# Transformer block with routed experts on one core: a setup that waits only for the front loop's loads, x loaded and its first norm taken inside it, the attention branch's weights split beside the routing, and a zero fill read from one row

## The chip, the cores and the metric

One of a Trainium2 chip's eight cores runs the kernel. Its engines are TensorE (PE in the rows), VectorE (DVE), ScalarE (ACT), GpSimd (POOL) and SyncE (SP), which here only issues transfers. The metric is the device time of one execution in microseconds, the median of several runs; lower is better.

## What is computed

`x` is 4 sequences of 2048 tokens with 256 features, 8192 tokens in all. The core of the reference normalises it and feeds it to two branches:

```python
xn = _layernorm(x, axis=-1)
s = _L0_attn_ref(xn, ...)     # linear attention, convolution, MLP of 1024
g = _silu(_L0_ffn_ref(xn, ...))   # attention over the 4 sequences' tokens, then 16 experts
x = x + s * g
```

`_L0_ffn_ref` takes a layer norm of `xn`, projects it to q, k, v (16 heads, 4 key/value heads), attends among the four tokens that share a position, projects and adds, takes a second layer norm `ln2`, and computes 16 router logits per token. Each token goes to its two best experts, into a slot of a buffer with 1280 slots per expert (unused slots are zero); each expert is an MLP 256 to 512 to 256; the results are weighted with the routing's probabilities and added. `_L0_attn_ref` needs `Wq, Wk, Wv`, `Wphi_q, Wphi_k`, a grouped convolution `conv_w` scaled by `gamma`, and an MLP `W1` (256x1024), `W2` (1024x256). All is float32.

## The kernel before

The program is written by hand, engine by engine, in blocks. Within a block each engine runs its own list, and semaphores tie the lists together; at the end of a block all engines meet before the next one starts. `Chain` makes each step of a list wait for the one before it. The blocks are, in order:

1. **Setup** (lines 264 to 424). SP issues 20 loads, then 16 small ones that place `conv_w` block by block into `wconv` (line 340); ScalarE issues 13 loads of vectors (line 353). All 33 count on one semaphore, `loaded`. POOL clears `wconv`, `brow2` and `zeros`, loads `wrouter`, and builds ten masks. VectorE waits for `loaded` and for the masks (`masks_made`), makes `bcast` and `one_rows` (lines 399 to 401), and TensorE computes sums of weight columns from them (lines 377 to 388); when all are done (`sums_made`), VectorE folds norm weights and means into `wqkv` and `wrouter` (lines 413, 414) and builds rows of biases `brow`. The weights of the attention branch are split into a high and a low part for exact products: `w_hi` by ScalarE, `w_lo = w - w_hi` by VectorE (`wa`, `w1`, lines 420, 422) or POOL (`w2`, line 310). POOL also scales `wconv` by `gamma` (line 306) and adds the identity (line 308), and scales `wphi` (line 314). Last, SP copies the split biases into `brow2` (lines 345, 346).
2. **Front loop** (lines 477 to 803), 16 turns, each with 4 x 128 tokens (one tile of each sequence). It is software-pipelined: in turn t, VectorE takes the statistics of x(t) (`front_stats`, lines 723 and 726), POOL turns them into the scale and shift of the two norms in eight steps (`norm`, lines 504 to 522), ScalarE applies them a turn later (`xn`, line 562, `xn_twice`, line 584), TensorE transposes and projects (line 708), and the attention among four tokens and the second norm follow two to four turns behind. SP loads x(t) into one of two buffers (line 484) once ScalarE is done with x(t-2), and after each x it issues one sixteenth of the zero fill of the experts' buffer `buf_d`, from a tile `zeros` of 128 x 10 x 272 (line 486). Each row of 272 holds 256 features and tags, one of which is a mark for an empty slot.
3. **Routing** (lines 827 to 898). VectorE alone finds the two best experts of all 8192 tokens in 13 steps on 128x1024 tiles, up to `chosen` (line 873); TensorE counts; VectorE computes slots. ScalarE takes two exponentials. POOL has no work.
4. **Attention branch** for sequences 0 and 1 with the scatter of tokens to the experts, **experts**, and the attention branch for sequences 2 and 3 with the final mix.

Before the routing's end, nothing of block 4 uses `wa_s`, `w1_s`, `w2_s`, `wphi`, `wconv` or `b1c`. `xnb` (128 x 16 x 256) holds normed rows of the attention branch; its first four tiles are written at the front loop's end.

The code that sets what a turn of the feed does:

```python
                            if later(t, 2):
                                sp.wait_ge(xn_made, t.n * S - S)
                            sp.dma_start(x[t.odd][:], rows_of(a["x"], t)).then_inc(x_in[t.odd], 16)
```

## Time and profile before

| | us |
|---|---|
| median of 3 runs | 2023.04 (2022.46 to 2023.44) |
| the profiled execution, its own time | 2030.76 |
| its span in the trace | 2029.0 |
| setup, up to the front loop's first issue | 48.0 |
| first `xn` of the front loop | 58.07 |
| routing, first step of VectorE | 366.39 |
| routing, last step of VectorE | 393.98 |

The trace is of one execution. Its own time is 1.8 us more than its span (what lies around the first and the last instruction) and 7.7 us more than the median of the runs. Times in the rows count from the span's start. An engine's busy time says what it worked, not what the others waited for; for that one reads which wait ended last in a stretch.

### The profile page before, as it was taken

To read this page: it belongs to the slowest core of one execution; us is meant where nothing else is said; L and a number is where in the kernel's file an instruction comes from. 1 tells how busy PE (TensorE), PEld (TensorE's weight loads), DVE (VectorE), ACT (ScalarE), POOL (GpSimd) and SP (SyncE) were. 2 spreads that over 40 slices of the span, in tenths; PEclk is the share of its full clock that TensorE was granted. 3 is DMA by queue.
4 is the path that set the end of the run, shared out by engine and by line. 5 is a ranking of instruction groups with operands and counts; after the bars stand their busy time and mean duration, and the time that the engine had idled before them with its cause. 6 is when DMAs were issued, how large, how long until landed. Compare 5 with 4: busy or idle time off the path is not lost. (4 is left out here: it accounts for less than half of the span.)

```text
span 2029.0 us, 37231 instructions
## 1 busy us (share of the span) xinstructions
PE 1812.5 (89%) x12776; PEld 1620.9 (80%) x12776; DVE 1375.7 (68%) x3573; ACT 817.8 (40%) x1945; POOL 962.0 (47%) x1500
## 2 busy tenths in 40 slices
PE   2699998399999999996999999999888999998998
PEld 2377776285898867996999999999875799875998
DVE  2698885654556535553777778877567588794786
ACT  1466664163323553321333333333355333572332
POOL 4466663175555564553656656566342233330431
PEclk9999999599999998997999999999989999998999
DMA  3454432123333123332333343332145022361122
GB/s 97 186 181 174 171 138 74 51 76 114 139 131 129 62 96 126 114 131 84 110 115 124 100 135 126 94 122 74 48 123 177 22 79 65 111 196 31 53 66 63
DMA packets 163510, 218.29 MB, mean 108 GB/s; under 512 B 22874, under 2 KB 144931, under 8 KB 161294
## 3 DMA queue, kind: packets, MB, share of 16 engines
q1 hardware_dynamic: 140574, 166.61, 25.7%
q0 software_dynamic: 18464, 49.49, 6.9%
q8 instruction: 97, 1.59, 0.3%
q10 hardware_dynamic: 4304, 0.02, 0.1%
q14 instruction: 71, 0.58, 0.1%
HBM read 114.94 MB, written 107.22 MB: 109 GB/s over the span
## 5 line engine op out<-in xcount | busy, mean ns | idle before, releaser
L1840 POOL DMA_INDIRECT picked_d<-h,home x160 | 163.6, 1022 | 192.3 <-DVE h L1887 156.7
L1766 ACT ACTIVATE hid<-bank 128x512 f32<-128x512 f32 x160 | 95.6, 598 | 336.1 <-PE bank L130 336.1
L128 PE MATMUL bank<-rows_hi,up_hi 128*128 128x256 f32 x640 | 189.0, 295 | 11.9 <-POOL up_lo L1834 7.6
L130 PE MATMUL bank<-rows_hi,up_lo 128*128 128x256 f32 x640 | 182.5, 285 | 0.0
L129 PE MATMUL bank<-rows_lo,up_hi 128*128 128x256 f32 x640 | 182.3, 285 | 0.0
L130 PE MATMUL bank<-down_hi,hid_lo 128*128 128x256 f32 x640 | 181.2, 283 | 0.0
L129 PE MATMUL bank<-down_lo,hid_hi 128*128 128x256 f32 x640 | 181.1, 283 | 0.0
L128 PE MATMUL bank<-down_hi,hid_hi 128*128 128x256 f32 x640 | 181.1, 283 | 0.0
L1170 POOL DMA_INDIRECT buf_d<-lt,to_row x128 | 134.4, 1050 | 86.4 <-POOL lt L1166 43.4
L1469 PE MATMUL bank<-wconv,knt 128*128 128x128 f32 x1280 | 157.1, 279 | 0.0
L1901 DVE TENSOR_TENSOR hid_lo<-hid,hid_hi 128x512 fp32r<-128x512 f32 x160 | 119.1, 753 | 52.6 <-ACT hid_hi L1766 49.8
L1469 PEld LDWEIGHTS bank<-wconv,knt 128*128 128x128 f32 x1280 | 152.6, 196 | 0.0
L1152 POOL TENSOR_SCALAR cnorm<-cmv 128x1 f32<-128x1 f32 x64 | 15.0, 235 | 289.9 <-DVE cmv L1672 289.0
L129 PE MATMUL bank<-w_lo,gel_hi 128*128 128x256 f32 x512 | 147.5, 288 | 0.0
L128 PE MATMUL bank<-w_hi,gel_hi 128*128 128x256 f32 x512 | 147.3, 288 | 0.0
L130 PE MATMUL bank<-w_hi,gel_lo 128*128 128x256 f32 x512 | 147.2, 288 | 0.0
L128 PE MATMUL bank<-ant_hi,w_hi 128*128 128x256 f32 x512 | 145.5, 284 | 0.0
L1334 ACT ACTIVATE tk<-bank,b1c 128x256 f32<-128x256 f32 x256 | 107.1, 471 | 90.4 <-PE bank L130 87.7
L129 PE MATMUL bank<-ant_lo,w_hi 128*128 128x256 f32 x512 | 143.0, 279 | 0.0
L130 PE MATMUL bank<-ant_hi,w_lo 128*128 128x256 f32 x512 | 142.9, 279 | 0.0
L1691 DVE TENSOR_TENSOR gel_lo<-tk,gel_hi 128x256 fp32r<-128x256 f32 x256 | 128.8, 503 | 8.8
L128 PEld LDWEIGHTS bank<-rows_hi,up_hi 128*128 128x128 f32 x640 | 124.1, 194 | 13.0 <-POOL up_lo L1834 8.0
(314 smaller groups left out, 5585.6 us busy)
## 6 DMA issues: line engine op xcount, KB each, us to landing
buf_d<-zeros SPq DMA_DIRECT2D x16, 1360.0 KB, 7.0
rows_in<-buf_d SPq DMA_DIRECT2D x80, 272.0 KB, 2.8
lt<-ln_d SPq DMA_DIRECT2D x128, 128.0 KB, 2.2
picked_d<-nothing SPq DMA_DIRECT2D x32, 512.0 KB, 3.3
job_picked<-picked_d SPq DMA_DIRECT2D x64, 256.0 KB, 2.9
x<-in_x SPq DMA_DIRECT2D x16, 512.0 KB, 4.3
after_d<-after SPq DMA_DIRECT2D x16, 512.0 KB, 2.9
ln_d<-ln SPq DMA_DIRECT2D x16, 512.0 KB, 2.8
```

The source lines that it names most:

```text
L128: pe.matmul(dst, hi, mhi, start=start and i == 0, stop=False)
L129: pe.matmul(dst, hi, mlo, start=False, stop=False)
L130: mm = pe.matmul(dst, lo, mhi, start=False, stop=end)
L1152: step.also(pool.tensor_scalar(n[3], mv_[0], -1.0, None, ALU.mult))
L1170: pool.indirect_dma_start(buf_d, bass.IndirectOffsetOnAxis(to_row[:, job, k:k + 1], axis=0), lt[p][:, k], None, bounds_check=SLOTS - 1, oo ...
L1334: act.activation(gel[:, f % 4], bank[f // 2 % 2][:, f % 2 * PAIR * P:(f % 2 + 1) * PAIR * P], ACT.Gelu, bias=b1c[:, f:f + 1]).then_inc(gel ...
L1469: mm = pe.matmul(conv[:, j * P:(j + 1) * P], attnt[:, j, k * P + tap:k * P + tap + P], wconv[:, j, tap], start=False, stop=j == 1 and tap ...
L1691: dve.tensor_tensor(lo[:, f], gel[:, f % 4], hi[:, f], ALU.subtract).then_inc(gel_split, 1)
L1766: act.activation(dst[:, 2 * half:2 * half + 2].rearrange("p f c -> p (f c)"), bank[half][:], ACT.Gelu_apprx_tanh).then_inc(e_hid, 1)
L1840: pool.indirect_dma_start(picked_d, bass.IndirectOffsetOnAxis(home[i % TAG_RING][:, r:r + 1], axis=0), h2[p][:, r], None, bounds_check=PIC ...
L1901: dve.tensor_tensor(lo[:, part], hid[p][:, part], hi[:, part], ALU.subtract).then_inc(hid_split, 1)
```

## The change

* **Loads.** They are reordered and count on three semaphores: `front_in` (`wqkv`, `wproj`, four vectors), `small_in` (19: `wphi`, biases, `gamma`, the other vectors) and `loaded` (8: `wa`, `w1`, `w2`, three rows). x(0) is loaded first of all and x(1) after the small ones, so that the loop's SP list issues x only from turn 2 on (`if later(t, 2)`).
* **Setup.** VectorE waits for `front_in` and two steps of POOL; it takes the statistics of x(0) there, and POOL its norm (`norm_twice`, the eight steps of lines 504 to 522 as a function), ahead of clearing `brow2` and `zeros`. Turn 0 of the loop has no statistics and no norm.
* **Splits.** The work on `wa`, `w1`, `w2`, `wphi`, `wconv` and `b1c` moves into the routing's block: ScalarE and TensorE do what they did; POOL does all four kinds of its own and both splits that were VectorE's. `w1` and `wa` stay in memory until then; `w2` lies in the last eight tiles of `xnb`.
* **Zero fill.** `zeros` is one row of 272 per partition, and the transfer reads it ten times.

```diff
-        zeros = sb("zeros", [P, CAP // P, ROW], into=front_only)
-        tags_made, zero_fill = sem("tags_made"), sem("zero_fill")
+        zeros = sb("zeros", [P, ROW], into=front_only)
+        zero_fill = sem("zero_fill")
+        w1 = sb("w1", [P, HALVES, MLP], into=front_only)
+        w2 = xnb[:, BT - MLP // P:BT]
+        wa = sb("wa", [P, HALVES, 3 * E], into=front_only)
+        gamma = sb("gamma", [P, 1], into=front_only)
+        x = [sb(f"x{p}", [P, S, E], into=front_only) for p in range(2)]
+        stats = sb("stats", [P, S, 6], into=front_only)
+        mv = [sb(f"mv{p}", [P, S, 2], into=front_only) for p in range(2)]
+        norm = [sb(f"norm{p}", [P, 8, S], into=front_only) for p in range(2)]
+        x_in = [sem("x_in0"), sem("x_in1")]
+        x_stats, x_mv, x_norm = sem("x_stats"), sem("x_mv"), sem("x_norm")
+        loaded, conv_in, pool_step = sem("loaded"), sem("conv_in"), sem("pool_step")
+        act_step, wa_high, sums_made = sem("act_step"), sem("wa_high"), sem("sums_made")
+        X_NORM = 8
+        LOADS, FRONT_LOADS, SMALL_LOADS, MASK_STEPS = 8, 6, 19, 20
...
-            LOADS = 33
...
-                    pool.memset(wconv[:], 0.0).then_inc(conv_blank, 1)
-                    pool.memset(brow2[:].bitcast(F32), 0.0).then_inc(rows_blank, 1)
-                    pool.memset(zeros[:], 0.0).then_inc(zeroed, 1)
-                    pool.wait_ge(zeroed, 1)
-                    pool.memset(zeros[:, :, E + 1], float(FAR)).then_inc(zeroed, 1)
...
-                    for t in (ident, diag, headmask, headmask_t, tri, earlier, ones_f, ones_b):
-                        step(pool.memset(t[:], 1.0))
-                    step(pool.memset(neg_half[:], -0.5))
-                    step(pool.memset(one_col[:], 1.0))
+                    for t in (ones_f, neg_half, ident, diag, headmask, headmask_t, tri, earlier, ones_b, one_col):
+                        step(pool.memset(t[:], -0.5 if t is neg_half else 1.0))
+                    pool.memset(wconv[:], 0.0).then_inc(conv_blank, 1)
...
+                              allow_small_or_imprecise_dtypes=True)
+                    assert step.done == MASK_STEPS
+                    pool.wait_ge(x_mv, S)
+                    norm_twice(pool, Chain(pool, x_norm), mv[0][:, :, 0], mv[0][:, :, 1], norm[0])
+                    pool.memset(brow2[:].bitcast(F32), 0.0).then_inc(rows_blank, 1)
+                    pool.memset(zeros[:], 0.0).then_inc(zeroed, 1)
+                    pool.wait_ge(zeroed, 1)
+                    pool.memset(zeros[:, E + 1:E + 2], float(FAR)).then_inc(zeroed, 1)
...
+                    def load(dst, src, done):
+                        sp.dma_start(dst, src).then_inc(done, 16)
+
+                    sp.dma_start(x[0][:], rows_of(a["x"], Step(0, 0))).then_inc(x_in[0], 16)
+                    load(wqkv[:], a["qkv_t"].rearrange("(j p) n -> p j n", p=P), front_in)
+                    load(wproj[:], a["proj_t"].rearrange("(j p) n -> p j n", p=P), front_in)
+                    load(wphi[:, 0], a["Wphi_q"].rearrange("(j p) n -> p j n", p=P), small_in)
+                    load(wphi[:, 1], a["Wphi_k"].rearrange("(j p) n -> p j n", p=P), small_in)
+                    for i, name in enumerate(("bq", "bk", "bv")):
+                        load(brow[:, i * E:(i + 1) * E], row(a[name]), small_in)
+                    for i, name in enumerate(("bphi_k", "conv_b", "lna_b", "b2")):
+                        load(extra[:, i * E:(i + 1) * E], row(a[name]), small_in)
+                    load(gamma[:], a["gamma"].to_broadcast((P, 1)), small_in)
+                    sp.dma_start(x[1][:], rows_of(a["x"], Step(0, 1))).then_inc(x_in[1], 16)
                     for i, name in enumerate(("Wq", "Wk", "Wv")):
+                        load(wa[:, :, i * E:(i + 1) * E], a[name].rearrange("(j p) n -> p j n", p=P), loaded)
+                    load(w1[:], a["W1"].rearrange("(j p) n -> p j n", p=P), loaded)
+                    load(w2, a["W2"].rearrange("(j p) n -> p j n", p=P), loaded)
                     for dst, name in ((gv_row, "lnv_g"), (bv_row, "lnv_b"), (ga_row, "lna_g")):
+                        load(dst[:], row(a[name]).to_broadcast((P, E)), loaded)
...
-                    act.wait_ge(loaded, 16 * LOADS)
+                    act.wait_ge(small_in, 16 * SMALL_LOADS)
                     act.activation(phik_zero[:], bphi[:, 1], ACT.Tanh).then_inc(phi_zero, 1)
-
-                    step = Chain(act, act_step)
-                    step(act.activation(w2_s[0][:], w2[:], ACT.Copy))
-                    act.activation(wa_s[0][:], wa[:], ACT.Copy).then_inc(wa_high, 1)
-                    act.wait_ge(sums_made, 1)
-                    for j in range(HALVES):
-                        step(act.activation(w1[:, j], w1[:, j], ACT.Copy, scale=lna[:, 0, j:j + 1]))
-                    step(act.activation(w1_s[0][:], w1[:], ACT.Copy))
...
-                        pe.matmul(bank[1][:, 0:P], bcast[:, 1, j], wrouter[:, j], start=j == 0, stop=j == 1)
+                        last = pe.matmul(bank[1][:, 0:P], bcast[:, 1, j], wrouter[:, j], start=j == 0, stop=j == 1)
+                    last.then_inc(sums_made, 1)
+                    pe.wait_ge(small_in, 16 * SMALL_LOADS)
...
-                    dve.wait_ge(loaded, 16 * LOADS)
+                    dve.wait_ge(front_in, 16 * FRONT_LOADS)
                     dve.wait_ge(router_in, 16)
-                    dve.wait_ge(masks_made, 1)
...
+                    dve.wait_ge(x_in[0], 16)
+                    for k in range(S):
+                        dve.bn_stats(stats[:, k], x[0][:, k]).then_inc(x_stats, 1)
+                    dve.wait_ge(x_stats, S)
+                    for k in range(S):
+                        dve.bn_aggr(mv[0][:, k], stats[:, k]).then_inc(x_mv, 1)
...
+                    dve.wait_ge(small_in, 16 * SMALL_LOADS)
+                    dve.wait_ge(sums_made, 2)
...
-                    dve.wait_ge(wa_high, 1)
-                    dve.tensor_tensor(wa_s[1][:], wa[:], wa_s[0][:], ALU.subtract).then_inc(wa_high, 1)
-                    dve.wait_ge(act_step, 4)
-                    dve.tensor_tensor(w1_s[1][:], w1[:], w1_s[0][:], ALU.subtract).then_inc(w1_split, 1)
...
-                            sp.dma_start(x[t.odd][:], rows_of(a["x"], t)).then_inc(x_in[t.odd], 16)
+                                sp.dma_start(x[t.odd][:], rows_of(a["x"], t)).then_inc(x_in[t.odd], 16)
 
                             sp.dma_start(buf_d.rearrange("(x p n) e -> p x n e", x=NX, p=P)[:, bass.ds(t.n, 1)]
-                                         .rearrange("p x n e -> p (x n) e"), zeros[:]).then_inc(zero_fill, 16)
+                                         .rearrange("p x n e -> p (x n) e"),
+                                         zeros[:].unsqueeze(1).to_broadcast((P, CAP // P, ROW))).then_inc(zero_fill, 16)
...
+                @block.gpsimd
+                def _(pool):
+                    step = Chain(pool, pool_step, MASK_STEPS)
+                    pool.wait_ge(loaded, 16 * LOADS)
+                    pool.wait_ge(wa_high, 1)
+                    pool.tensor_tensor(wa_s[1][:], wa[:], wa_s[0][:], ALU.subtract).then_inc(wa_high, 1)
+                    for i, g in enumerate((lnq, lnk)):
+                        for j in range(HALVES):
+                            step(pool.tensor_scalar(wphi[:, i, j], wphi[:, i, j], g[:, 0, j:j + 1], None, ALU.mult))
+                    pool.wait_ge(conv_in, 16 * H)
+                    step(pool.tensor_scalar(wconv[:], wconv[:], gamma[:, 0:1], None, ALU.mult))
+                    for j in range(HALVES):
+                        step(pool.tensor_tensor(wconv[:, j, 2], wconv[:, j, 2], ident[:], ALU.add))
+                    pool.wait_ge(act_step, 1)
+                    step(pool.tensor_tensor(w2_s[1][:], w2, w2_s[0][:], ALU.subtract))
+                    pool.wait_ge(act_step, 4)
+                    step(pool.tensor_tensor(w1_s[1][:], w1[:], w1_s[0][:], ALU.subtract))
+
                 @block.tensor
                 def _(pe):
+                    pe.wait_ge(loaded, 16 * LOADS)
+                    for n in range(MLP // P):
+                        for j in range(HALVES):
+                            last = pe.matmul(bank[4][:, n:n + 1], w1[:, j, n * P:(n + 1) * P], lna[:, 1, j:j + 1],
+                                             start=j == 0, stop=j == 1)
+                    last.then_inc(sums_made, 1)
...
+                    step = Chain(act, act_step)
+                    act.wait_ge(loaded, 16 * LOADS)
+                    act.activation(wa_s[0][:], wa[:], ACT.Copy).then_inc(wa_high, 1)
                     act.wait_ge(route_step, SHIFTED)
                     act.activation(odds[:], logit, ACT.Exp).then_inc(odds_made, 1)
+                    step(act.activation(w2_s[0][:], w2, ACT.Copy))
                     act.wait_ge(route_step, SECOND + 1)
                     act.activation(second[:], second[:], ACT.Exp).then_inc(second_made, 1)
+                    act.wait_ge(sums_made, 3)
+                    for j in range(HALVES):
+                        step(act.activation(w1[:, j], w1[:, j], ACT.Copy, scale=lna[:, 0, j:j + 1]))
+                    step(act.activation(w1_s[0][:], w1[:], ACT.Copy))
...
+                    dve.wait_ge(sums_made, 3)
+                    step(dve.tensor_tensor(b1c[:], bank[4][:, 0:MLP // P], b1c[:], ALU.add))
```

POOL's list. The setup before, from its second wait for the loads to its end (`w` is `w2`, `bank` a PSUM bank):

```order
L301 IOTA rank_e 128x16 [waits pool_step]
L306 TENSOR_SCALAR wconv<-wconv,gamma 128x1280 [waits conv_in,loaded]
L308 TENSOR_TENSOR wconv<-wconv,ident 128x128 [waits pool_step] x2
L310 TENSOR_TENSOR w_lo<-w,w_hi 128x2048 [waits act_step,pool_step]
L314 TENSOR_SCALAR wphi<-wphi,lnq 128x256 [waits sums_made,pool_step]
L314 TENSOR_SCALAR wphi<-wphi,lnq 128x256 [waits pool_step]
```

and after, the whole of POOL's list in the routing's block, which was empty before:

```order
L828 TENSOR_TENSOR wa_lo<-wa,wa_hi 128x1536 [waits wa_high,loaded]
L831 TENSOR_SCALAR wphi<-wphi,lnq 128x256
L831 TENSOR_SCALAR wphi<-wphi,lnq 128x256 [waits pool_step]
L831 TENSOR_SCALAR wphi<-wphi,lnk 128x256 [waits pool_step] x2
L833 TENSOR_SCALAR wconv<-wconv,gamma 128x1280 [waits conv_in,pool_step]
L835 TENSOR_TENSOR wconv<-wconv,ident 128x128 [waits pool_step] x2
L837 TENSOR_TENSOR w_lo<-xnb,w_hi 128x2048 [waits act_step,pool_step]
L839 TENSOR_TENSOR w_lo<-w,w_hi 128x2048 [waits act_step,pool_step]
```

The rows of the setup stand in the routing with both subtracts of VectorE's added: `wa_lo` first, the one of `w1` last (the name `xnb` is the place of `w2`).

VectorE's list in the setup before:

```order
L399 TENSOR_SCALAR bcast<-ones_f,ln1b,ln1w 128x128 [waits masks_made,router_in,loaded]
L401 CAST one_rows<-ones_f 128x128 [waits setup_step]
L404 COPY router_bias<-bank 128x16 [waits sums_made,setup_step]
L408 TENSOR_SCALAR brow<-extra,gamma 1x256 [waits setup_step]
L409 TENSOR_TENSOR brow<-extra 1x256 [waits setup_step]
L414 SCALAR_TENSOR_TENSOR wqkv<-bank,wqkv 128x384 [waits setup_step]
L416 CAST brow_hi<-brow 1x1536 [waits setup_step]
L418 TENSOR_TENSOR brow_lo<-brow,brow_hi 1x1536 [waits rows_split]
L420 TENSOR_TENSOR wa_lo<-wa,wa_hi 128x1536 [waits wa_high]
L422 TENSOR_TENSOR w_lo<-w,w_hi 128x2048 [waits act_step]
L424 TENSOR_SCALAR phik_zero<-phik_zero 128x2 [waits phi_zero]
```

and after:

```order
L406 TENSOR_SCALAR bcast<-ones_f,ln1b,ln1w 128x128 [waits pool_step,router_in,front_in]
L408 CAST one_rows<-ones_f 128x128 [waits setup_step]
L411 BN_STATS stats<-x 128x6 [waits x_in0,setup_step]
L414 BN_AGGR mv<-stats 128x2 [waits x_stats]
L417 COPY router_bias<-bank 128x16 [waits sums_made]
L421 SCALAR_TENSOR_TENSOR wqkv<-bank,wqkv 128x384 [waits setup_step]
L425 TENSOR_TENSOR phiq_bias<-bank,bphi 128x2 [waits sums_made,small_in,setup_step]
L427 TENSOR_SCALAR brow<-extra,gamma 1x256 [waits setup_step]
L428 TENSOR_TENSOR brow<-extra 1x256 [waits setup_step]
L429 CAST brow_hi<-brow 1x1536 [waits setup_step]
L431 TENSOR_TENSOR brow_lo<-brow,brow_hi 1x1536 [waits rows_split]
L433 TENSOR_SCALAR phik_zero<-phik_zero 128x2 [waits phi_zero]
```

The statistics of x stand where `one_rows` used to be followed by the wait for all sums; the two splits are gone; the wait for the small loads comes after the folds of `wqkv` and `wrouter`.

SP's list at the end of the setup and the start of the loop, after:

```order
L360 DMA brow<-brow_hi 1x16x96 [waits rows_blank,rows_split,zeroed]
L361 DMA brow<-brow_lo 1x16x96
L288 UNCONDITIONAL_BRANCH [waits row_two]
L478 UNCONDITIONAL_BRANCH [waits barrier_Pool_Activation_PE_DVE_SP_release]
L486 DMA buf_d<-zeros 1280x1x272 x2
L484 DMA x<-in_x 128x4x256 [waits xn_made]
L486 DMA buf_d<-zeros 1280x1x272
```

Before, the same two `brow` copies were followed by `x`, fill, `x`, fill, and the fill's form was 128x2720.

## Rows read from the trace of the kernel before

**Rows 1.** The page, busy time of each engine.

```profile
PE 1812.5 (89%) x12776; PEld 1620.9 (80%) x12776; DVE 1375.7 (68%) x3573; ACT 817.8 (40%) x1945; POOL 962.0 (47%) x1500
```

**Rows 2.** By stage: start:end, length, busy PE, PEld, DVE, ACT, POOL; PEclk, DMA share, GB/s.

```profile
0.00:48.00 48.00, 13.99 (x52) 11.22 (x52) 12.63 (x22) 8.97 (x7) 24.69 (x39) 1.00 0.37 96
110.00:200.00 90.00, 87.85 (x474) 65.68 (x473) 79.55 (x215) 59.54 (x127) 54.19 (x99) 1.00 0.50 180
366.30:382.70 16.40, 0.00 (x0) 0.00 (x0) 15.90 (x13) 1.31 (x2) 0.00 (x0) 0.50 0.00 0
```

**Rows 3.** Timeline of ScalarE, first `xn` and two turns: start, length, line, operation.

```profile
58.07 2.07 ACT L562 ACTIVATE xn<-x,norm 128x256 f32<-128x256 f32 x4 [17.94 <-POOL norm L505]
...
104.33 2.08 ACT L562 ACTIVATE xn<-x,norm 128x256 f32<-128x256 f32 x4 [2.01 <-PE bank L646]
...
120.97 2.08 ACT L562 ACTIVATE xn<-x,norm 128x256 f32<-128x256 f32 x4 [2.11 <-PE bank L646]
```

**Rows 4.** Waits up to 62 us: who waited for whom, us.

```profile
PE bank L377 <- DVE one_rows L401: 21.8, 1, 21.8
...
DVE bcast L399 <- DMA ga_row<-in_lna_g: 20.1, 1, 20.1
...
SPq L344 <- DVE brow_lo L418: 20.2, 1, 20.2
```

**Rows 5.** Timeline of VectorE, setup and first turns.

```profile
45.17 2.27 DVE L422 TENSOR_TENSOR w_lo<-w,w_hi 128x2048 fp32r<-128x2048 f32 x1
...
52.14 1.41 DVE L723 BATCH_NORM_STATS2 stats<-x 128x6 f32<-128x256 f32 x4 [3.73 <-DMA x<-in_x]
...
70.43 1.40 DVE L723 BATCH_NORM_STATS2 stats<-x 128x6 f32<-128x256 f32 x4
```

**Rows 6.** Timeline of the SP queue: last large load, `wconv`, second `brow` copy, first x.

```profile
12.58 0.43 SPq L320 DMA_DIRECT2D ga_row<-in_lna_g  x1
13.06 10.30 SPq L340 DMA_DIRECT2D wconv<-in_conv_t  x16
...
44.28 0.59 SPq L346 DMA_DIRECT2D brow<-brow_lo  x1
48.01 0.39 SPq L484 DMA_DIRECT2D x<-in_x  x1
```

**Rows 7.** Transfers up to 12 us by queue, and up to 62 us by issue (last: us to landing).

```profile
q1 hardware_dynamic: 2137, 2.86, 71.4%
...
buf_d<-zeros SPq DMA_DIRECT2D x3, 1360.0 KB, 7.0
...
x<-in_x SPq DMA_DIRECT2D x3, 512.0 KB, 4.2
...
brow<-brow_lo SPq DMA_DIRECT2D x1, 6.0 KB, 1.8
```

**Rows 8.** Timeline of TensorE in the setup, the first and the last sums.

```profile
21.83 2.93 PE L377 MATMUL bank<-wqkv,bcast 128*128 128x384 f32 x4 [21.83 <-DVE one_rows L401]
...
28.84 6.99 PE L388 MATMUL bank<-lna,w 128*128 128x1 f32 x32
```

**Rows 9.** Timeline of POOL in the setup, and of VectorE beside its last rows.

```profile
24.98 3.57 POOL L306 TENSOR_SCALAR wconv<-wconv,gamma 128x1280 f32<-128x1280 f32 x1 [10.90 <-DMA wconv<-in_conv_t]
...
29.70 4.51 POOL L310 TENSOR_TENSOR w_lo<-w,w_hi 128x2048 fp32r<-128x2048 f32 x1
36.00 2.04 POOL L314 TENSOR_SCALAR wphi<-wphi,lnq 128x256 f32<-128x256 f32 x2 [1.79 <-PE bank L388]
...
37.37 0.50 DVE L409 TENSOR_TENSOR brow<-extra 1x256 f32<-1x256 f32 x1
```

**Rows 10.** Timeline of VectorE, then of POOL, in the expert stage.

```profile
1062.88 0.69 DVE L1880 TENSOR_TENSOR rows_lo<-rows_t,rows_hi 128x512 fp32r<-128x512 f32 x1
...
1069.78 2.77 DVE L1880 TENSOR_TENSOR rows_lo<-rows_t,rows_hi 128x512 fp32r<-128x512 f32 x1
...
1069.47 2.53 POOL L1834 TENSOR_TENSOR down_lo<-down_w,down_hi 128x1024 fp32r<-128x1024 f32 x1
```

**Rows 11.** Timeline of VectorE in the routing: the 2nd and 13th of 13 steps.

```profile
367.65 1.22 DVE L860 TENSOR_REDUCE highest<-logits 128x64 f32<-128x1024 f32 x1
...
381.47 1.22 DVE L873 TENSOR_TENSOR chosen<-hot 128x1024 bf16<-128x1024 f32 x1
```

97 lines of the change are left out of this document (30 added, 67 removed).

## The prediction

> **What bounds the kernel now.** I read the engine totals first. TensorE is busy 89% of the span [rows 1], so most of the 2029 us is its work and stays out of this change, which touches three stretches only: the setup, the front loop's feed and the routing. A table by stage shows how they differ [rows 2]. In the first 48 us no engine is busy for more than 25 us: this stretch is bounded by waits. In the front loop (110 to 200 us) TensorE is busy 87.85 of 90 us: there only TensorE's work counts, and a turn takes 120.97 - 104.33 = 16.64 us [rows 3]. In the routing's first 16.4 us VectorE is busy 15.90 us, POOL (GpSimd) not at all and TensorE not at all: VectorE is the bound, alone.
>
> Next, the waits of the setup. VectorE starts only at 20.14 us, when the last of all 33 loads has landed; TensorE at 21.83 us; the sync queue waits 20.2 us for `brow_lo` [rows 4]. VectorE's last long step is the split of W1, 45.17 to 47.44 us [rows 5], and the next block's first load is issued at 48.01 us [rows 6]. From there the first norm is a bare chain: x lands, statistics at 52.14 us [rows 5], POOL's eight small steps, and ScalarE's first `xn` at 58.07 us [rows 3]. That is 10.06 us in which only one thing happens at a time.
>
> **The change, part by part.**
>
> *Term 1, the end of the setup.* VectorE now waits for six loads, ahead of which stands only x: 512 + 384 + 256 KB, 1.18 MB. In the first 12 us the sync queue moved 2.86 MB [rows 7], so these should land at about 8 to 9 us (2 us until traffic flows, 1.18 / 0.286 = 4.1 us, some 2 us to landing, which is the 1.8 us of the tiny `brow_lo` transfer [rows 7]). What follows is short: VectorE's busy time in the whole setup was 12.63 us [rows 2], of which the splits of Wa and W1 leave (2.27 us the larger one [rows 5]), so even with the new statistics (under 2 us), TensorE's first sums, 21.83 to 25.6 us before, and its two small products, 3.6 us more up to 28.84 us [rows 8], VectorE is through at about 22 to 23 us. POOL had 24.69 us of work [rows 2]; 3.57 us of `wconv`, about 1 us of its identity, 4.51 us of W2's split and 4.04 us of `wphi` leave [rows 9], about 2 us of zeroing go with the smaller tile, 4 us of norm come: about 16 us of work with one wait, through at 20 us. So neither of them ends the setup. **The sync queue does**: its loads were all issued at 13.0 us [rows 6], with two x loads of 0.4 us more at 13.9 us; the 16 small `wconv` loads take 10.30 us of issuing [rows 6], to 24.2 us; the two `brow` copies take 0.6 us each, the second is issued at 24.8 us, lands 1.8 us later [rows 7] at 26.6 us, and from there to the next block's first issue it was 48.01 - 47.5 = 0.5 us. That is 27.1 us. The two x loads add 1.05 MB to a queue that was full when it issued; at 0.286 MB per us that is up to 3.7 us more of waiting. I take 0.5 us of it, since most of it is drained while the `wconv` loads are issued: 27.6 us, a gain of 20.4 us (bounds 17 to 21).
>
> *Term 2, the first norm.* It is now ready before the block starts, at about 13 us by VectorE and 17 us by POOL, below the setup's end. ScalarE's first `xn` starts as the block does, at 27.7 us instead of 58.07 us. Terms 1 and 2 together: -30.4 us. If the setup ends late, the second term stays at 10.0.
>
> *Term 3, the third x.* The first two turns of the new loop issue the zero fills alone, and x for turn 2 comes behind both, about 2.2 us after the block starts (when four `xn` are made). Its statistics were taken at 70.43 us [rows 5], 12.36 us after the first `xn`. A fill landed after 7.0 us and x after 4.2 us beside it [rows 7]. Two fills are 2.8 MB; as 2560 pieces at 64 ns on 16 queues (the setup's mean piece: 0.714 x 16 x 12 us / 2137 [rows 7]) they take 10.2 us, x 2 us more and landing 2 us: 14.7 us against 12.4. By the rate at which the larger pieces flowed it is in time. I take 1.0 us late (0 to 3).
>
> *Term 4, the splits beside the routing.* All of Wa, W1, W2, `wphi` and `wconv` now lies in the block where VectorE alone is the bound. ScalarE's part and TensorE's 16 sums (6.99 us for both halves, at most twice that at the granted clock of 0.50 that this stretch has [rows 2, 8]) run beside it and end before the 16.4 us are over: hidden, nothing queued behind them. POOL's part is not free, though POOL sits idle there. In the expert stage VectorE's `rows_lo`, two inputs in SBUF, takes 0.69 us; issued 0.3 us into POOL's subtract of 128x1024 it took 2.77 us and ended 0.5 us after POOL's [rows 10]. So it didn't run slower, it stood still. Of VectorE's 13 steps up to `chosen` nine are of that kind, 1.22 us each, and four are reduces with one input [rows 11]; the front loop's reduces don't stretch beside POOL. POOL's two-input steps here are `wa_lo`, 1536 columns at 4.51 / 2048 us [rows 9], 3.4 us; `wconv` plus identity, 2 x 0.45; `w2_lo` and `w1_lo`, 4.51 us each: 13.3 us. I lay them beside VectorE's steps (times from the block's start; `chosen` ended at 16.3 before). `wa_hi` is ready at 1.5, so `wa_lo` runs 1.6 to 4.95; VectorE's reduce ends at 2.5, and its next step waits to 4.95: 2.4 us lost. `wphi` and `wconv`, one input each, run to 12.8; the two identity steps cost 0.3. `w2_lo` runs 15.6 to 20.1, VectorE waits from 16.5: 3.6 lost. `w1_lo` has waited behind VectorE's step and takes its turn at 21.3, to 25.8: `chosen` waits, 4.4 lost. Sum 10.7 us, and 0.2 for `b1c` at the end: **+10.9 us** (bounds 0 if the steps don't stop one another here, and 13.5 if every us of it is lost).
>
> The Trainium skill, "SBUF — State Buffer", section "SBUF: two separate sides", says that the pair of ports which VectorE shares with GpSimd is an exclusive lock, held for the whole instruction, and it names any GpSimd instruction as a holder, not the two-input ones alone. By that rule POOL's one-input steps would stop VectorE too. The trace agrees on the two-input case with its 2.77 us [rows 10].
>
> What would one-input steps cost? `wphi` (4 x 0.98) and `wconv` (3.57) laid in the same way move `chosen` from 27.0 to 32.0: +5 us. The one row that bears on it speaks against: VectorE's two-input `brow` on `extra` ran from 37.37 to 37.87 us, inside a `wphi` step of POOL's that went on to 38.04 [rows 9]; 0.50 us is no stall of that length. I leave it out.
>
> *The fill from one row* changes nothing in the steady loop: 1280 pieces of 1088 bytes at 64 ns are 5.1 us of the queues in a turn of 16.64 us, where all traffic took half the time [rows 2]. The loads moved in order, the smaller memsets and the wait by `loaded` inside the routing cost nothing: all long landed.
>
> **Sum.** -30.4 + 1.0 + 10.9 = -18.5 us. The profiled execution took 2030.76 us, so 2012.3 us; the median of the runs is 7.7 us below it, 2023.04, so 2004.5 us is forecast. A measurement tells about 0.2% (4 us) from nothing.
>
> **The rivals.**
> 1. *No stall in the routing*, because the two-input steps meet mostly reduces, or because broadcast operands (most of the routing's) don't take the port. For it: in the front loop POOL's and VectorE's small steps alternate at little cost. Against: 2.77 us [rows 10]. It gives 2004.5 - 10.9 = 1993.6 us.
> 2. *Every POOL step stops VectorE*: 2004.5 + 5.0 = 2009.5 us.
> 3. *The setup ends late*: the change doesn't deliver its early start, since the loads it waits for share the 16 queues with all that is issued behind them, and the `wconv` loads and `brow` copies queue behind 1.05 MB more. The queues' data then ends 3.7 us later, and with the third x 2 us later than taken: 2010 us.
> 4. *The fill binds the loop* (the other side). 128 pieces of 10,880 bytes become 1280 of 1088. All traffic takes 8.3 us of a turn now; to lose the 18.5 us and 4 more, the turn must reach 16.64 + 22.5 / 16 = 18.0 us, so the fill would need 9.7 us more, 121 ns per piece. It decides from there; the setup's pieces took 64 ns. At 150 ns a turn takes 8.3 + 12 = 20.3 us, 59 us more in 16 turns: 2064 us.
>
> **How the numbers follow.** Forecast 0.62 (its own range 2000 to 2009). Rival 1: 0.13. Rival 2: 0.13. Rival 3: 0.08. Rival 4: 0.04. The range 1992.5 to 2012.5 holds the first four but for their tails. Only the fill can undo the gain, and a mild case of it would land near no change: faster 0.96, same 0.01, slower 0.03.
>
> **What would show it.** Step 1: the loop's first fill is issued near 27.6 us, right after the second `brow` copy has landed. Step 2: ScalarE's first `xn` within 0.3 us of it, and no idle before it. Step 3: VectorE's third statistics wait for x, by 0 to 3 us. Step 4: `chosen` ends 27 us after the routing's start, with three VectorE steps of 3.6, 4.8 and 5.6 us in place of 1.22, each ending 1.2 us after a POOL subtract. The forecast is wrong in its reasons if those steps stay at 1.22 us, if a reduce stretches, if the turn isn't 16.6 us, or if the expert stages' times move.

## The result, and the profile after

| | before | after |
|---|---|---|
| median of 15 runs each, us | 2022.46 (2015.51 to 2029.54) | 2013.95 (2009.12 to 2018.82) |
| profiled execution: its own time, span | 2030.76, 2029.0 | 2010.27, 2008.5 |
| front loop's first issue | 48.01 | 32.27 |
| first `xn` | 58.07 | 32.29 |
| routing, VectorE's first step | 366.39 | 343.26 |
| attention branch, TensorE's first product | 394.76 | 383.81 |

The changed kernel takes 0.9956 of the time before, 95% interval 0.9943 to 0.9969: 8.9 us less (6.3 to 11.5), where 18.5 us less was forecast. Runs of one kernel lie up to 18 us apart (2014.14 to 2032.53 us for the kernel before, beside run 1), and in the traces of all kernels here the time behind the attention branch's first product is between 1619 and 1634 us, whatever the kernel. So the two profiled executions, 20.5 us apart, are compared only up to that product. Up to there the change gains 394.76 - 383.81 = 10.95 us, in line with the medians: 25.8 up to the first `xn`, less 2.65 lost in the loop (308.32 us from first `xn` to routing before, 310.97 after), less 12.2 in the routing (28.37 us, now 40.55).

Busy time of each engine after (against [rows 1]), from the page:

```profile
PE 1806.9 (90%) x12775; PEld 1616.4 (80%) x12776; DVE 1382.0 (69%) x3571; ACT 818.0 (41%) x1945; POOL 968.5 (48%) x1502
```

By stage after: setup, a stretch of the loop, the routing up to `chosen` (against [rows 2], same columns):

```profile
0.00:32.20 32.20, 7.28 (x20) 4.32 (x20) 10.08 (x27) 1.49 (x2) 13.57 (x39) 0.77 0.63 175
110.00:200.00 90.00, 86.28 (x459) 63.78 (x458) 78.94 (x214) 58.39 (x124) 56.44 (x101) 1.00 0.55 176
343.20:371.60 28.40, 6.96 (x32) 6.90 (x32) 27.90 (x14) 8.69 (x7) 24.91 (x10) 0.50 0.00 1
```

In the loop TensorE is busy for 86.28 of 90 us, 1.6 us less than before. In the routing VectorE still seems fully busy, in 28.4 us for the work of 16.4: a stopped step counts as busy.

**The setup.** The SP queue (against [rows 6]), then TensorE ([rows 8]), VectorE ([rows 5]) and ScalarE ([rows 3]), from the timelines of after:

```profile
12.19 3.48 SPq L333 DMA_DIRECT2D gv_row<-in_lnv_g  x1
...
16.70 10.34 SPq L355 DMA_DIRECT2D wconv<-in_conv_t  x16
...
30.07 0.59 SPq L361 DMA_DIRECT2D brow<-brow_lo  x1
32.27 1.53 SPq L486 DMA_DIRECT2D buf_d<-zeros  x2
34.40 2.25 SPq L484 DMA_DIRECT2D x<-in_x  x1
```

```profile
10.87 2.93 PE L386 MATMUL bank<-wqkv,bcast 128*128 128x384 f32 x4 [10.87 <-DVE one_rows L408]
...
21.37 1.87 PE L393 MATMUL bank<-lnq,wphi 128*128 128x1 f32 x8 [6.90 <-DMA b1c<-in_b]
```

```profile
9.18 0.34 DVE L406 TENSOR_SCALAR bcast<-ones_f,ln1b,ln1w 128x128 f32<-128x128 f32 x1 [9.18 <-DMA ln2b<-in_ln_bias]
...
27.62 1.75 DVE L431 TENSOR_TENSOR brow_lo<-brow,brow_hi 1x1536 fp32r<-1x1536 f32 x1
...
45.13 0.56 DVE L735 COPY qkv<-bank 128x384 f32<-128x384 f32 x1 [10.61 <-PE bank L703]
45.60 1.40 DVE L718 BATCH_NORM_STATS2 stats<-x 128x6 f32<-128x256 f32 x4
```

```profile
10.29 0.49 ACTq L370 DMA_DIRECT2D b1c<-in_b  x1
...
32.29 1.09 ACT L557 ACTIVATE xn<-x,norm 128x256 f32<-128x256 f32 x2 [10.74 <-PEq L288]
```

VectorE starts at 9.18 us, and the third statistics (45.60) follow a copy with no wait. But TensorE's small products wait to 21.37 us: `b1`, 4 KB in 1024 pieces, is the last load that ScalarE issues and one of the 19 in `small_in` that they wait for. `brow_lo` is ready only at 29.37 us, and SP, done with `wconv` at 27.04 us, copies it after that.

**The routing.** VectorE and POOL after (against [rows 11] and [rows 9]):

```profile
345.77 3.61 DVE L888 TENSOR_TENSOR logits<-logits,highest 128x1024 f32<-128x1024 f32 x1
349.41 1.38 DVE L890 SCALAR_TENSOR_TENSOR ranked<-logits,rank_e 128x1024 f32<-128x1024 f32 x1
350.83 1.22 DVE L891 TENSOR_REDUCE rank<-ranked 128x64 f32<-128x1024 f32 x1
...
356.01 2.72 DVE L896 TENSOR_TENSOR ranked<-place,second 128x1024 f32<-128x1024 f32 x1
...
361.42 4.70 DVE L899 TENSOR_TENSOR hot<-rank_e,rank 128x1024 f32<-128x1024 f32 x1
366.15 5.40 DVE L900 TENSOR_TENSOR chosen<-hot 128x1024 bf16<-128x1024 f32 x1
```

```profile
344.87 3.43 POOL L828 TENSOR_TENSOR wa_lo<-wa,wa_hi 128x1536 fp32r<-128x1536 f32 x1 [4.03 <-ACT wa_hi L867]
348.27 3.32 POOL L831 TENSOR_SCALAR wphi<-wphi,lnq 128x256 f32<-128x256 f32 x2
...
354.19 3.92 POOL L833 TENSOR_SCALAR wconv<-wconv,gamma 128x1280 f32<-128x1280 f32 x1
...
360.52 4.51 POOL L837 TENSOR_TENSOR w_lo<-xnb,w_hi 128x2048 fp32r<-128x2048 f32 x1
365.11 5.36 POOL L839 TENSOR_TENSOR w_lo<-w,w_hi 128x2048 fp32r<-128x2048 f32 x1
```

Three steps end 1.1 us after a subtract of POOL's (348.30, 365.03, 370.47 us). A fourth, 2.72 us, ends 0.62 us after the one-input `wconv`; beside `wphi` a step takes 1.38 us; the reduces keep 1.22 us. Beside `wphi` it is mostly POOL that waits: the two steps of 3.32 us together took 2.04 in the setup of before [rows 9].

### The profile page after: what moved, and what is told of

Its sections match the earlier page's. It is cut to its first block and busy times, and to the rows that moved or that the text cites. A ratio compares the mean times of both kernels' runs of the same rounds, so it can differ in the third digit from the quotient of the medians.

```text
span 2008.5 us, 37232 instructions
## 1 busy us (share of the span) xinstructions
PE 1806.9 (90%) x12775; PEld 1616.4 (80%) x12776; DVE 1382.0 (69%) x3571; ACT 818.0 (41%) x1945; POOL 968.5 (48%) x1502
```

## The experiments

All edits are to the changed kernel unless said. "Attention" is the time of the attention branch's first product: 394.76 us before, 383.81 after.

### 1. The subtracts by VectorE at the routing's end

```diff
-                    pool.tensor_tensor(wa_s[1][:], wa[:], wa_s[0][:], ALU.subtract).then_inc(wa_high, 1)
...
+                    step(dve.tensor_tensor(wa_s[1][:], wa[:], wa_s[0][:], ALU.subtract))
+                    step(dve.tensor_tensor(w2_s[1][:], w2, w2_s[0][:], ALU.subtract))
+                    step(dve.tensor_tensor(w1_s[1][:], w1[:], w1_s[0][:], ALU.subtract))
```

> The changed kernel with the three subtracts (wa, w2, w1) taken from POOL and made by VectorE after its last routing step; POOL keeps its one-input steps and the two identity adds. Theory A (POOL's long two-input steps stop VectorE's): the three stretched steps (3.61, 4.70, 5.40 us in the changed kernel) come back to 1.2 to 1.4 us, VectorE adds 1.7 + 2 x 2.3 = 6.3 us at the end, and from the routing's first step to the attention branch's start it takes 28.4 + 1.2 + 0.2 + 6.3 = 36.1 us instead of 40.55; about 4.4 us faster than the changed kernel. Rival B (the stretch comes from ScalarE's or TensorE's work beside it, or from one-input steps): the steps stay at 3.6 to 5.4 us, and the stage takes 46 us or more.

VectorE's, then POOL's timeline of this kernel:

```profile
346.50 1.23 DVE L881 TENSOR_TENSOR logits<-logits,highest 128x1024 f32<-128x1024 f32 x1
...
350.42 3.74 DVE L885 TENSOR_TENSOR hot<-rank_e,rank 128x1024 f32<-128x1024 f32 x1
...
361.87 1.23 DVE L893 TENSOR_TENSOR chosen<-hot 128x1024 bf16<-128x1024 f32 x1
```

```profile
350.02 3.52 POOL L830 TENSOR_SCALAR wconv<-wconv,gamma 128x1280 f32<-128x1280 f32 x1
```

The steps stretched by the subtracts are back at 1.23 us: the subtracts were the cause. What is left is one step of 3.74 us beside `wconv`, 2.5 us lost, again ending 0.62 us after it. The stage takes 381.80 - 343.98 = 37.82 us (40.55 in after), with the subtracts' 6.34 us on VectorE; the 36.1 us expected had no such step. The total can't be told from the change's: 2013.44 us, ratio 0.9944 (0.9923 to 0.9964).

### 2. The one-row fill alone, in the kernel before

```diff
-        zeros = sb("zeros", [P, CAP // P, ROW], into=front_only)
+        zeros = sb("zeros", [P, ROW], into=front_only)
...
-                                         .rearrange("p x n e -> p (x n) e"), zeros[:]).then_inc(zero_fill, 16)
+                                         .rearrange("p x n e -> p (x n) e"),
+                                         zeros[:].unsqueeze(1).to_broadcast((P, CAP // P, ROW))).then_inc(zero_fill, 16)
```

> The kernel before with the zero fill read from one row and nothing else. Theory A (the fill form is free): setup and first xn where they were (48.0 and 58.1 us), turns of 16.3 to 17.3 us as before, the third statistics not waiting for x, first routing step at 366.4 us within 0.5. Rival B (the fill's small pieces lengthen each turn by about 0.15 us): the first routing step comes 1.6 to 2.4 us later, with a higher DMA share in the front loop (0.55 against 0.50).

From 110 to 200 us, columns as in [rows 2]:

```profile
110.00:200.00 90.00, 88.00 (x474) 65.74 (x473) 79.65 (x214) 59.92 (x128) 55.32 (x101) 1.00 0.54 176
```

TensorE is as busy as before (87.85 us) and the queues carry 0.54 in place of 0.50: from the second on, all turns agree with those of before within 0.02 us. The fill's form is free. The first `xn` came at 55.61 us here, 2.5 us sooner than in the profiled execution of before. Its loads were in 1.45 us sooner, and TensorE's 32 sums, 6.99 us there [rows 8], took 5.32 us: part of the 25.8 us gained up to the first `xn` is one slow setup. It lost 1.3 us of this in the loop's first turn and 1.3 behind the last turn's first `xn`, and attention came at 394.80 us, as before. The granted clock was 0.50 in the first (55.6 to 65.6 us) and 0.54 in a part of the second (337.4 to 342.4 us), and both stretches differ by as much between runs with the one-row fill, so this is not put down to the fill.

### 3 and 4. `b1` not waited for in the setup; then `wconv` loaded in the loop as well

```diff
-        LOADS, FRONT_LOADS, SMALL_LOADS, MASK_STEPS = 8, 6, 19, 20
+        LOADS, FRONT_LOADS, SMALL_LOADS, MASK_STEPS = 9, 6, 18, 20
...
-                            act.dma_start(dst, col(a[name])).then_inc(front_in if name in FRONT_VECTORS else small_in, 16)
+                            act.dma_start(dst, col(a[name])).then_inc(
+                                front_in if name in FRONT_VECTORS else loaded if name == "b1" else small_in, 16)
```

Run 4 adds:

```diff
-                    for g in range(H):
-                        c = D * (g % 8)
-                        sp.dma_start(wconv[c:c + D, g // 8, :, c:c + D], a["conv_t"][g]).then_inc(conv_in, 16)
...
+                            if isinstance(t.n, int) and t.n == 3:
+                                for g in range(H):
+                                    c = D * (g % 8)
+                                    sp.dma_start(wconv[c:c + D, g // 8, :, c:c + D], a["conv_t"][g]).then_inc(conv_in, 16)
```

> The changed kernel with the load of b1 (1024 pieces of 4 bytes, the last that ScalarE issues) counted with the late loads instead of the small ones. Theory A (this load held TensorE's two small products from 14.5 to 21.35 us): they start near 16 us, brow_lo ends near 24 us, before the sync queue has issued wconv (27.0 us); the brow copies go at 27.1 instead of 29.45 us and the loop starts near 29.9 instead of 32.27 us, 2.4 us earlier. Rival B (all small loads land late together, since they share the 16 queues with the large ones behind them): the products start at 20 us or later and the loop's start moves by under 1 us.

> As the run before this one, and the 16 wconv loads issued in the front loop's fourth turn, behind its fill, instead of ahead of the brow copies. Theory A (the sync queue's issuing bounds the setup's end once b1 no longer does): the brow copies go as brow_lo ends, near 24 us, the loop starts near 26.7 us, 5.5 us earlier than in the changed kernel; the turns keep their length. Rival B (VectorE's chain still ends the setup at 29 us): the loop's start stays within 1 us of the run before this one.

Timelines of run 3, TensorE, VectorE and SP:

```profile
15.84 1.05 PE L394 MATMUL bank<-lnq,wphi 128*128 128x1 f32 x8 [1.20 <-DMA bphi<-in_bphi_k]
...
21.13 1.75 DVE L432 TENSOR_TENSOR brow_lo<-brow,brow_hi 1x1536 fp32r<-1x1536 f32 x1
...
26.83 0.58 SPq L360 DMA_DIRECT2D brow<-brow_hi  x1
...
29.65 1.52 SPq L487 DMA_DIRECT2D buf_d<-zeros  x2
```

and run 4, SP:

```profile
23.74 0.67 SPq L356 DMA_DIRECT2D brow<-brow_hi  x1
...
26.63 1.53 SPq L483 DMA_DIRECT2D buf_d<-zeros  x2
```

Without `b1` the products start at 15.84 us, `brow_lo` is ready at 22.9 us, and the loop starts at 29.65 us, now held by SP's `wconv` loads; without these it starts at 26.63 us. So the 32.27 us of the change are 26.6, 3.0 for SP behind `wconv`, and 2.6 for `b1`. Theory A holds in both, within 0.3 us. Attention: 382.12 and 379.17 us; one run each, 2011.28 and 2005.19 us, too few to be compared.

### 5 and 6. The splits in the loop's last turns; then with the setup of run 4

TensorE's sums go to turns 1 and 2, ScalarE's part and POOL's `wphi` and `wconv` to the loop's last turns (its tail), and VectorE takes the subtracts there, where it waits for `xa`. The routing's block has the routing alone, as before.

```diff
...
+                    dve.wait_ge(wa_high, 1)
+                    dve.tensor_tensor(wa_s[1][:], wa[:], wa_s[0][:], ALU.subtract).then_inc(wa_low, 1)
+                    dve.wait_ge(act_step, 4)
+                    dve.tensor_tensor(w1_s[1][:], w1[:], w1_s[0][:], ALU.subtract).then_inc(wa_low, 1)
+                    dve.tensor_tensor(w2_s[1][:], w2, w2_s[0][:], ALU.subtract).then_inc(wa_low, 1)
...
```

> The changed kernel with the splits moved once more, from the routing into the front loop's last turns, where VectorE, POOL and ScalarE wait: ScalarE makes the high parts at turn 18, POOL scales wphi and wconv there, VectorE makes all three subtracts after its last statistics (9 us of idle, 6.3 us of work), TensorE computes b1's sums in turns 1 and 2. The routing's block holds the routing alone. Theory A (the routing stage was lengthened by the shared port and by nothing else): all 13 steps up to chosen take 1.22 us, the stage is 28.4 us again (it was 40.55), setup and turns stay, the attention branch starts near 372 us, 12 us earlier than in the changed kernel. Rival B (the splits only move their cost: the loop's last turns lengthen by what the routing gains): the routing's first step comes 6 us or more later than 343.3 us.

> The run before this one with the setup of the fourth run (b1 counted late, wconv loaded in the loop). If the gains add (setup 5.6 us, routing 12.2 us): the attention branch starts near 366 us, 18 us earlier than in the changed kernel and 29 us earlier than before; a ratio to the kernel before near 0.986. If they don't, one of the two stages has a bound that was hidden by the other.

Run 6, VectorE:

```profile
315.16 1.73 DVE L838 TENSOR_TENSOR wa_lo<-wa,wa_hi 128x1536 fp32r<-128x1536 f32 x1
316.80 2.28 DVE L840 TENSOR_TENSOR w_lo<-w,w_hi 128x2048 fp32r<-128x2048 f32 x1
319.00 2.29 DVE L841 TENSOR_TENSOR w_lo<-xnb,w_hi 128x2048 fp32r<-128x2048 f32 x1
329.00 0.43 DVE L208 BATCH_NORM_STATS2 xstats<-xa 128x6 f32<-128x256 f32 x1 [7.71 <-DMA xa<-in_x]
...
336.18 1.23 DVE L900 TENSOR_TENSOR logits<-logits,router_bias 128x1024 f32<-128x1024 f32 x1 [1.72 <-PEq L475]
...
351.28 1.22 DVE L914 TENSOR_TENSOR chosen<-hot 128x1024 bf16<-128x1024 f32 x1
```

Run 6, POOL and ScalarE beside the subtracts, and ScalarE at the same place of after:

```profile
315.41 1.56 POOL L507 TENSOR_SCALAR norm<-mv 128x4 f32<-128x4 f32 x1 [2.05 <-DVE mv L758]
317.05 2.93 POOL L508 TENSOR_TENSOR norm<-norm,neg_half 128x4 f32<-128x4 f32 x1
```

```profile
321.71 1.93 ACT L640 ACTIVATE ln<-bank,norm 128x256 f32<-128x256 f32 x4 [5.32 <-POOL norm L539]
```

```profile
328.94 1.93 ACT L617 ACTIVATE ln<-bank,norm 128x256 f32<-128x256 f32 x4 [0.96 <-POOL norm L527]
```

In the tail the subtracts look free, since VectorE still waits 7.71 us for `xa`, but they are not: they make `xa` come later. POOL's steps for the last norm fall beside them and take 1.56, 2.93 and 1.29 us (0.23, 1.04 and 0.20 in after); ScalarE's `ln` waits for these, and SP issues `xa` behind the store of `ln`, 8.8 us after VectorE's last statistics and means (324.08 - 315.24), where in after it is 4.4 us (331.31 - 326.86). So they cost 4.4 us, by these waits; no run has the subtracts alone taken out of the tail. From the last turn's first `xn` to the routing it takes 63.54, 62.99 and 63.59 us in runs 5, 6 and 9, and 57.5 to 59.8 us in the other eleven traces.

In run 5 the turns from the second to the last won 5.84 us (see below; 238.92 us in after, 233.08 here), and the tail lost 6.01 of it (57.53 us, 63.54 here). So the routing starts at 343.55 us, as Theory A has it, but by luck: it says that the turns stay and has no loss in the tail. Of the routing's block it is right, all 13 steps take 1.22 or 1.23 us again; of the tail rival B is right in part, 6.0 of its 12 us.

From the routing's start to attention both runs take 28.38 us, as before. Run 5: attention 371.93 us, 2002.37 us, ratio 0.9890 (0.9859 to 0.9921). Run 6: 364.56 us, 1994.74 us, ratio 0.9860 (0.9826 to 0.9894). It beats both kernels (the change, timed beside it as run 7: 2011.27 us), and takes 394.76 - 364.56 = 30.2 us off the front.

An unexpected thing paid as well: in both runs every turn from the seventh on took 16.6 to 16.7 us, where before's alternate between 16.91 and 17.29 and after's, from the eighth on, between 17.37 and 17.29. (The program writes out the first six turns and the last four, which only finish what is under way; the ten between are rolled, a body of two turns that runs five times.)

### 7, 8, 11 and 12. What sets the turn: one tiny step on POOL

In a turn VectorE multiplies `early` (three steps) when POOL begins `weighed` (seven). A turn of after, VectorE then POOL:

```profile
175.50 2.02 DVE L772 TENSOR_TENSOR early<-qkv,prob 128x256 f32<-128x256 f32 x3 [0.17 <-DVE prob L766]
```

```profile
175.81 4.61 POOL L536 TENSOR_TENSOR weighed<-qkv,prob 128x256 f32<-128x256 f32 x7 [0.37 <-POOL norm L527]
```

Run 7 is the change itself, a control. Run 8 puts a meaningless step in front of `weighed`:

```diff
+            idle = sb("idle", [P, S], F32, own)
...
+                            pool.tensor_tensor(idle[:], neg_half[:], neg_half[:], ALU.mult)
                             for i, (s, u) in enumerate(PAIRS[3:]):
```

> The changed kernel itself once more, as a control for the stage times. If what comes before the attention branch is fixed by the program: first xn within 0.5 us of 32.3, the routing stage 40.5 us, the attention branch's start within 1 us of 383.8 but for TensorE's clock in the loop's first turn (1.0 to 1.3 us). If the remaining stages vary from run to run: they take 1624 to 1634 us, as in the runs so far, whatever the kernel.

> The changed kernel with one small POOL step (128x4, about 0.2 us) ahead of its seven `weighed` steps in each turn. Theory A (in the rolled turns `weighed` starts 0.1 us earlier than in the kernel before and so takes the shared port ahead of one more of VectorE's three `early` steps): `early` takes 1.55 us in every second turn again instead of 2.01, those turns 16.9 instead of 17.37 us, the loop about 2 us shorter although POOL does more. Rival B (the longer turns come from something else): the turns stay at 17.3 to 17.4 us.

Run 7 came out as expected, with attention at 384.70 us (2011.27 us, ratio 0.9935 (0.9915 to 0.9956)). In run 8 attention came at 376.80, 7.9 us sooner, where Theory A had some 2 us: `early` fell in the rolled turns not to 1.55 us but to 1.10. Its one timed run took 2003.21 us. So both were timed once more side by side, as runs 11 and 12:

> The eighth run's kernel again (the changed kernel with one two-input 128 x 4 step on POOL ahead of `weighed` in every turn), now timed against the kernel before beside the unchanged change. Theory A (the loop's gain is kept to the end): rolled turns of 16.6 us, attention's first product at 376.5 to 377.5 us, ratio 0.991 to 0.993, which is 6 to 8 us below the change in the same rounds. Rival (what the front gains is lost again behind it, as the tenth run's total with its 8 us earlier attention suggests): the same turns, but a ratio within 0.001 of the change's.

> The changed kernel as it is, a control for the run beside it. Both theories: rolled turns alternating near 17.4 and 17.3 us, attention's first product at 383.8 to 384.7 us, ratio 0.9935 to 0.996.

Run 11, VectorE then POOL:

```profile
171.78 1.10 DVE L774 TENSOR_TENSOR early<-qkv,prob 128x256 f32<-128x256 f32 x3 [0.17 <-DVE prob L768]
```

```profile
172.66 0.27 POOL L535 TENSOR_TENSOR idle<-neg_half 128x4 f32<-128x4 f32 x1 [0.37 <-POOL norm L528]
172.89 4.45 POOL L538 TENSOR_TENSOR weighed<-qkv,prob 128x256 f32<-128x256 f32 x7
```

`weighed` now starts as `early` ends, and `early` takes 1.10 us, not 2.02. From the seventh on, turns take 16.61 to 16.67 us (in run 12 the seventh 16.81, those behind it 17.28 to 17.39), attention is at 376.25 us (384.48), and the total 2003.90 us, ratio 0.9916 (0.9896 to 0.9937), against 2012.88 us, 0.9948 (0.9931 to 0.9965). Theory A holds, and its gain is kept to the end; the rival of run 11 falls. Runs 5 and 6 agree without any added step: in their rolled turns from the seventh on `weighed` starts 0.9 us after `early`, which takes 1.10 us, in place of 0.3 us after it. What moved it there stays open.

This holds for the rolled turns. In the written-out fourth and fifth turns of after `early` takes 2.00 us as well, and the turns take 16.64 and 16.60 us (16.42 and 16.37 in run 11, with 1.10 and 1.54 us).

### 9 and 10. The same step in the best kernel, and in the kernel before

> The sixth run's kernel (splits in the loop's tail, b1's load no longer waited for ahead of the loop, wconv loaded in the loop) with the eighth run's delay: one two-input 128 x 4 step on POOL ahead of `weighed` in every turn. Theory A (the order in which POOL's `weighed` and VectorE's `early` come to their data sets the turn): the sixth run's written-out turns, of which several took 16.9 to 17.3 us, fall to 16.4 to 16.6, while the rolled ones already took 16.6, so the gain over the sixth run is small: first xn at 26.3 us, attention's first product at 362 to 364.5 us (the sixth run: 364.56), ratio to the kernel before 0.983 to 0.987. Rival: the delay only helps where the turn was disturbed, and an added step in a turn that is already at 16.6 us lengthens it: by the added step's length, up to 0.1 us in each of 20 turns, attention's first product at 365 to 367 us and a ratio of 0.986 to 0.988.

> The kernel before, with nothing but the delay step (one two-input 128 x 4 step on POOL ahead of `weighed` in every turn). Theory A: the kernel before already paid for the order in every second turn (its turns alternate 16.91 and 17.29 us), so all rolled turns come to 16.6 us here: from the first xn to routing's start 303 to 305 us in place of 308.3, setup and routing unchanged (first xn 58.1 us; routing to attention 28.4 us), attention's first product at 390 to 391.5 us in place of 394.8, ratio 0.9975 to 0.9985. Rival: the gain of the eighth run came out of the changed setup's loop alone, and the turns here stay at 16.9 and 17.3 us: attention's first product at 394.8 us, ratio 1.000.

All `early` steps of before, after, and run 10: shortest, median and longest ns.

```profile
L777 DVE TENSOR_TENSOR early<-qkv,prob x48: 415/644/892, 82.6 to 335.6; 128x256 f32<-128x256 f32 x48
```

```profile
L772 DVE TENSOR_TENSOR early<-qkv,prob x48: 415/860/903, 57.8 to 312.7; 128x256 f32<-128x256 f32 x48
```

```profile
L779 DVE TENSOR_TENSOR early<-qkv,prob x48: 410/420/867, 80.2 to 327.3; 128x256 f32<-128x256 f32 x48
```

From the sixth on run 10's turns take 16.60 to 16.67 us: before had paid for the same collision in part of its turns. From first `xn` to routing it takes 302.75 us (308.32), and attention comes at 386.51 us, sooner than expected because its first `xn`, at 55.39 us, is also 2.7 us sooner, with 32 sums of 5.41 us, and because the loop is a little shorter than the 303 to 305 us expected. The rival, which has the gain come out of the changed setup alone, falls. The total, 2021.14 us, ratio 0.9986 (0.9968 to 1.0004), can neither show nor exclude the 5.6 us. Run 9: attention 362.25 us, 2.3 us before run 6 (1.0 of it an earlier first `xn`, 25.28 us), total 1995.94 us, ratio 0.9866 (0.9840 to 0.9892): no difference from run 6 that can be measured, since its turns had little left to gain.

## Why the prediction was wrong

The sign was right, the size not: -18.5 us forecast, -10.95 up to attention in the traces and -8.9 (-6.3 to -11.5) in the medians. The 7.55 us between forecast and trace are 4.6 in the setup, 1.65 in the loop and 1.3 in the routing; all three cost more than forecast.

**Term 1, setup: failed, -15.7 us for -20.4 (the loop starts at 32.27 us, forecast 27.6).** The step that failed is "TensorE's first sums ... and its two small products, 3.6 us more ... VectorE is through at about 22 to 23 us": it gave the products a duration and no wait. The change makes them wait for 19 loads, and I priced the end of the six in `front_in` and of SP's issuing, never that of `small_in`. Its last member, `b1`, held TensorE's products to 21.37 us (15.84 without it) and `brow_lo` to 29.37 us; run 3 removes that and gains 2.6 us. There VectorE is through at 22.9 us, so the durations were right and the wait was missing. The second miss, the other 2.0 us, was SP: it reached `wconv` at 16.70 us, not 13.9, mostly since `gv_row` took 3.48 us to issue (0.43 in before) and the load of `Wk` 2.69 (0.47). Rival 3 (setup ends late, 0.08) had named the shared queues, but its 2010 us come from 3.7 us of queued data and a late third x, not from `b1`. POOL's work was added up wrongly, without effect: the terms give 13.6 us, not 16, and it worked 13.57.

**Term 2: right.** `xn` starts 0.02 us after the first fill, no norm before it. Its 10.0 us hold at either setup end.

**Term 3: wrong mechanism.** The third x is in time; the statistics wait for nothing. (The terms that lead to its 14.7 us, 10.2, 2 and 2, add up to 14.2.) The loop still loses 2.65 us (3.5 to 3.9 in runs 1, 3, 7 and 12, which have the change's loop), in two other places: 0.96 us in the first turn, 1.94 from the second to the last, less 0.25 behind them. The first turn takes 14.52 us (13.56): its 16 products on `wqkv` take 8.00 us (7.04 before) where the granted clock is 0.50 from 32 to 42 us (1.2 GHz; before, 1.00 from 58 to 68 us, 2.4 GHz). This is not the change's: run 7, the same kernel, has 1.00 there and a first turn of 13.64 us; run 2, with the setup of before, has 0.50, 8.34 us for the products and a first turn of 14.84 us; and all first turns lie between 13.4 and 14.9 us. The rest is the change's: every second rolled turn is slower, since POOL starts `weighed` about 0.1 us sooner in every second turn, where `early` loses another 0.46 us (2.01 for 1.55). The sentence "the front loop's reduces don't stretch" was true and beside the point; the loop's multiplies do stretch, and I had read one turn of 16.64 us from the written-out part, as if it stood for the 16.91 and 17.29 of the rolled one.

**Term 4, routing: right in its mechanism, +12.2 us for +10.9.** The steps forecast at 3.6, 4.8 and 5.6 us took 3.61, 4.70 and 5.40; `chosen` ended 28.3 us after the start, not 27.0. What I had set to nothing is the one step of 2.72 us beside `wconv` (1.5 us) and two of 1.38 us beside `wphi` (0.3 in all); the third near 1.37 us, beside the identity steps, cost half of the 0.3 us that it had. Run 1 shows `wconv`'s part by itself, 3.74 us. So rival 1 (no stall) is refuted, and rival 2 is right in part: the one-input steps cost 1.8 us, not 5.0. The Trainium skill, "SBUF — State Buffer", section "SBUF: two separate sides", has the first of the two to start hold the shared ports for its whole instruction, where VectorE's has two inputs in SBUF and GpSimd's reads SBUF. All of POOL's steps here read SBUF, those with one input too. The trace agrees for two-input steps; for one-input steps it agrees in part: `wconv` held a step of VectorE's back, though half of that step's own time had passed when it ended (0.62 of 1.22 us was left), and `wphi` cost 0.16 us beside steps of over 1.2 us. The row of `brow` beside `wphi` [rows 9] was read rightly (0.50 us there, 0.41 in after with POOL idle), and carried too far: to a step of 3.5 us.

**The fill: right.** Rival 4 is refuted by run 2.

**The range** ended at 2012.5 because the bounds of term 1 (17 to 21) knew only of SP's queue. And the base, one profiled execution, had a slow setup (48.01 us, with 6.99 us for the 32 sums; runs 2 and 10, which have the same setup but for the size of `zeros` in run 2, 45.40 and 45.27 us), which all of term 1 is counted from: against these two the setup gained 13.0 to 13.1 us, not 15.7.

## What to carry to other kernels

When a semaphore is split, price the last member of each new group, not the first that matters: a vector loaded in 4-byte pieces beside large loads can land long after its size says. Work moved under an engine that is alone at the bound is hidden only where its steps don't stop that engine's: here POOL's steps, 24.91 us of them as they ran, cost 12 us. An engine's idle time before a load isn't free either: the subtracts that VectorE made there stopped small steps of POOL's on the way to the load's issue, and cost 4.4 us. So ask of every idle stretch what the wait at its end hangs on. Where steps of two engines stop one another, the turn's length can depend on who arrives first; after any change of such a loop, compare rolled turns, and try a delay of a quarter of a microsecond on the engine with slack.
